# Attention with two copies of every query part: selection rows issued ahead of the moves, and all second score products over 68 rows

## The reference, cut to what matters

```
qe = einsum('hbtd,hde->hbte', q, Wq_exp) * mask      # 6 experts
ke = einsum('hbtd,hde->hbte', k, Wk_exp) * mask
attn = softmax(einsum('rbqhd,rbkhd->rbhqk', qe, ke) / D**0.5)
o = einsum('rbhqk,rbkhd->rbqhd', attn, v * mask)
o = einsum('rbthd,rbth->bthd', o, rw)                # weighted over the experts
o = (o * silu(g)) @ Wo
```

## Time and profile before

| what | us |
|---|---|
| median of 3 runs (lowest, highest) | 2963.82 (2961.93, 2968.57) |
| the profiled execution | 2963.52 |
| its span | 2961.8 |
| TensorE busy | 2509.6 (85%) |
| VectorE busy | 1791.9 (60%) |
| ScalarE busy | 1235.1 (42%) |
| GpSimd busy | 965.2 (33%) |
| DMA bytes | 441.60 MB |
| mean granted clock of TensorE | 0.914 |

### The profile page before, as it was taken

The page is one execution under the profiler, slowest core; times in us unless marked ns, Lnnn a source line. Parts: engine busy times, 40 slices in busy tenths (PEclk is TensorE's granted clock), DMA queues, the critical chain, the costliest instruction groups (busy, mean ns, idle before and its releaser), DMA issues. The chain is left out here.

```text
span 2961.8 us, 32540 instructions
## 1 busy us (share of the span) xinstructions
PE 2509.6 (85%) x9340; PEld 1655.3 (56%) x9340; DVE 1791.9 (60%) x2651; ACT 1235.1 (42%) x2450; POOL 965.2 (33%) x1004
## 2 busy tenths in 40 slices
PE   7999859999999998793799999267998865699989
PEld 5778724444444444570688888143454424588867
DVE  4310228989989998553455554448999996411143
ACT  3222027777777776231455554362233213311121
POOL 0102023333333331546100000317999994101010
PEclk9999969999999997886899999578999998899979
DMA  5253356565665661855677663634444445200031
GB/s 178 81 179 113 99 123 155 156 158 152 154 155 156 160 157 58 254 212 208 242 230 230 229 229 132 193 114 163 158 171 168 172 164 164 78 29 21 0 107 64
DMA packets 298210, 441.60 MB, mean 149 GB/s; under 512 B 41592, under 2 KB 124552, under 8 KB 298096
## 3 DMA queue, kind: packets, MB, share of 16 engines
q1 hardware_dynamic: 263392, 389.36, 43.3%
q10 hardware_dynamic: 28720, 33.10, 3.2%
q0 software_dynamic: 5984, 17.73, 1.8%
HBM read 303.85 MB, written 94.32 MB: 134 GB/s over the span
## 5 line engine op out<-in xcount | busy, mean ns | idle before, releaser
L1000 ACT ACTIVATE attn_probs<-attn_ps_score,attn_nmax 128x512 f32<-128x512 f32 x512 | 343.0, 673 | 5.6 <-DVE attn_nmax L1076 4.5
L2463 PE MATMUL scan_ps_o<-scan_qs,scan_sel 128*128 128x512 f32 x512 | 263.6, 631 | 80.5 <-DVE scan_qs L2407 53.4
L913 PE MATMUL attn_ps_score<-attn_KK,attn_S 128*128 128x512 f32 x512 | 278.8, 545 | 51.9 <-ACT attn_probs L1000 48.9
L2425 DVE TENSOR_TENSOR_SCAN scan_st<-scan_ps_dec,scan_kv 128x512 f32<-128x512 f32 x256 | 306.2, 1211 | 18.0 <-POOL scan_kv L2377 17.6
L913 PEld LDWEIGHTS attn_ps_score<-attn_KK,attn_S 128*128 128x128 f32 x512 | 101.2, 198 | 225.1 <-ACT attn_probs L1000 195.1
L841 POOL TENSOR_TENSOR attn_masked<-attn_spread,attn_q 128x512 f32<-128x512 f32 x96 | 122.7, 1281 | 294.9 <-DMA attn_spread<-rows 189.3
L2463 PEld LDWEIGHTS scan_ps_o<-scan_qs,scan_sel 128*128 128x128 f32 x512 | 88.7, 193 | 231.2 <-DVE scan_qs L2407 144.8
L1090 DVE SCALAR_TENSOR_TENSOR attn_mixed<-attn_probs,attn_cf,attn_mixed 128x512 f32<-128x512 f32 x256 | 197.2, 770 | 9.0
L1065 DVE TENSOR_REDUCE attn_raw<-attn_ps_score 128x2 f32<-128x1024 f32 x128 | 155.9, 1218 | 32.2 <-PE attn_ps_score L915 31.7
L1010 ACT ACTIVATE attn_probs<-attn_probs,attn_cf 128x512 f32<-128x512 f32 x128 | 92.4, 722 | 194.1 <-DVE attn_cf L1081 194.1
L2377 POOL TENSOR_TENSOR scan_kv<-scan_vb,gla_gk 128x512 f32<-128x512 f32 x128 | 161.2, 1277 | 19.6 <-DMA scan_vb<-gv 9.4
(11 more groups left out here) (434 smaller groups left out, 6391.3 us busy)
## 6 DMA issues: line engine op xcount, KB each, us to landing
scan_vb<-gv SPq DMA_DIRECT2D x256, 256.0 KB
moe_raw<-in_L_ffn_gating SPq DMA_DIRECT2D x92, 512.0 KB, 4.6
attn_spread<-rows SPq DMA_DIRECT2D x64, 384.0 KB, 8.8
moe_raw<-in_L_ffn_linear SPq DMA_DIRECT2D x46, 512.0 KB, 4.4
attn_S<-attn_X SPq DMA_DIRECT2D x64, 256.0 KB, 4.3
attn_S<-attn_Y SPq DMA_DIRECT2D x128, 128.0 KB, 4.3
rows_x<-out_zeros SPq DMA_DIRECT2D x23, 512.0 KB, 9.1
moe_xb<-rows_x SPq DMA_DIRECT2D x23, 512.0 KB, 5.9
```

The source lines that it names most:

```text
L913: nc.tensor.matmul(ps_score[n][:, j, :], S[p][:, 2 * n + j, cols], KK[p][:, :], start=True, stop=False)
L1000: nc.scalar.activation(probs[b][:, at_j, :], ps_score[n][:, j, :], ACT.Exp, bias=nmax[b][:, at_j:at_j + 1], accum_out=Z[b][:, at_j:at_j + ...
L2425: V.tensor_tensor_scan(st[r][:, :], ps_dec[n % 2][:, :], kv[r][:, :], 0.0, ALU.mult, ALU.add).then_inc(st_ready, 1)
L2463: nc.tensor.matmul(ps_o[w][:, :], sel[:, P - GPH - GPH * d:2 * P - GPH - GPH * d], qs[i % RING][:, :], start=(d == 0), stop=(d == HALF - 1 ...
```

## The change

The inputs of unit u + 3 are issued ahead of the mask rows and moves of u + 1. S gets two more slots, 6 and 7, for a second copy of the high parts of the shared experts; the transfer that moves a high part now always has two destinations. Partitions 64 to 67 of slots 6 and 7 are zeroed once and stay zero, so the 68-row product adds nothing there. All second products use 68 rows and S slots 4 to 7.

```diff
-        S = [m.sb(f"S{p}", [P, 6, T], F32R) for p in two]
+        S = [m.sb(f"S{p}", [P, 8, T], F32R) for p in two]
...
                 for j, half in enumerate((low, high)):
                     part = X[p][half, n, :].bitcast(F32)
-                    if n == AB:
-                        sp.dma_start(S[p][low, j:j + 5:4, :].bitcast(F32), part.unsqueeze(1).to_broadcast([DH, 2, T])
-                                     ).then_inc(sem, 16)
-                    else:
-                        sp.dma_start(S[p][low, 2 + j, :].bitcast(F32), part).then_inc(sem, 16)
+                    first_copy = 2 * n + j
+                    sp.dma_start(S[p][low, first_copy:first_copy + 5:4, :].bitcast(F32),
+                                 part.unsqueeze(1).to_broadcast([DH, 2, T])).then_inc(sem, 16)
...
             def step(i, p, u, first):
+                if left(u) >= 3:
+                    inputs(1 - p, u + 3, False)
                 if left(u) >= 1:
                     mask_rows(1 - p, u + 1, first and p == 0)
                     move(1 - p, u + 1, AB)
                     move(1 - p, u + 1, SHARED)
-                if left(u) >= 3:
-                    inputs(1 - p, u + 3, False)
                 if left(u) >= 2:
                     keys(p, u + 2, False)
...
-                ch.link(nc.gpsimd.memset(S[p][DH:DH + NSEL, 4:6, :].bitcast(F32), 0.0))
+                ch.link(nc.gpsimd.memset(S[p][DH:DH + NSEL, 4:8, :].bitcast(F32), 0.0))
...
                         nc.tensor.matmul(ps_score[n][:, j, :], S[p][:, 2 * n + j, cols], KK[p][:, :], start=True, stop=False)
-                        if n == AB:
-                            last = nc.tensor.matmul(ps_score[n][:, j, :], S[p][0:DH + NSEL, 4 + j, cols], KL[p][:, :],
-                                                    start=False, stop=True)
-                        else:
-                            last = nc.tensor.matmul(ps_score[n][:, j, :], S[p][low, 2 + j, cols], KL[p][low, :], start=False,
-                                                    stop=True)
+                        last = nc.tensor.matmul(ps_score[n][:, j, :], S[p][0:DH + NSEL, 4 + 2 * n + j, cols], KL[p][:, :],
+                                                start=False, stop=True)
```

## The result

The changed kernel takes 3026.22 us (median of 4 runs, 3014.03 to 3033.77) against 2964.38 for the kernel before in the same comparison: the ratio is 1.0204, 95% interval 1.0178 to 1.0231. It is 62 us slower. The prediction had +30 and a range that ended at 3004 (3010 for 8 in 10).

The account below looks back on a forecast made before the run. Two never-idle DMA engines, which alone carry q and k besides their share of all else, were taken to bound the attention stage. 2963.5 + 31.5 (copies) - 1 (TensorE) = 2994 us; range 2981 to 3004, for 8 in 10 2962 to 3010.

Parts of the forecast that it names:

- What bounds the kernel: Attention stage: two never-idle DMA engines, carrying q and k plus their sixteenth of all else, set 23.5 us per head.
- Part 1: Second copies of the shared experts' high parts, 2 x 128 KB more per head: 1.05 us in 30 heads, +31.5 us.
- Part 2: Inputs of head u+3 issued ahead of mask rows and moves: no byte of the two busy engines' work changes, 0 us.
- What would be late next: Moves into S would land late, so TensorE waits for S and VectorE for scores, 60 us or more; spread rows earlier.
- Part 3: TensorE's shared second products on 68 rows, 399 against 500 ns: 0 in the steady stretch, gain 0 to 2.5, taken 1 us.
- Part 4: Zeroing twice as many values of S at the start, some 1.9 us for 0.94, twice: cost 0 to 2, taken 0.
- Rival C: Attention stage: moves behind inputs leave TensorE idle at head starts, scores late by 1.45 us per head: +42, 3036; chance 0.07.
- Rival A: Attention stage: queue order is the mechanism; early spread rows end VectorE's stalls for Z: faster, 2921 to 2932 us; chance 0.13.
- the floor: One-microsecond windows of the attention stage: DMA share never under 0.12, read as two of 16 engines never idle.

Follow-up runs that it names:

- the groups: Kernel before plus 256 KB transfers by themselves, in seven groups ahead of the attention stage: 321 GB/s into 128 partitions, 205 to 208 into one half; 3043.1 us, not compared.

## Why the prediction was wrong, point by point

- What bounds the kernel: right. Two engines are never idle and a head takes their work. Splitting q and k took 2.6% off and brought heads to VectorE's 21.8 us.
- Part 1, the copies: right in mechanism and near in size. 31.5 us were predicted, 1.05 per head; the copies alone cost a ratio of 1.0103, 31 us (16 to 45), and 1.27 us per head. The profiled executions differ by 37.7 us, so that the total comes out within 1 us is in part luck: the price per head was a fifth too low. The value that I took lay just under the prices at 242 GB/s (1.08) and at the stage's average (1.07). By the slow rate that I had as the upper end, 199 GB/s, it is 1.32. The copies write one half, which in the groups was slow, and that would fit; no run shows it for the copies.
- Part 2, the order: this is the step that failed. "But the order changes no byte of the pair's work ... I take 0" is true of the bytes and false of the time. The order alone costs 0.9% and 1.44 us per head. My sum took one rate for the common work, from a trace in which it was 15.3 GB/s per engine, and carried it to another order, in which it is 13.8. That term of 0 measured 27 us by itself (18 to 35), and some 43 on top of the copies. The rows already spread from 199 to 280 GB/s at the same full share, and I used that spread only as bounds of the copies' price.
- What would be late next: wrong. I had the moves, with TensorE waiting for S. GpSimd's wait for spread rows is still the one that counts: 260.0 us, not under 50, and no wait of TensorE for S stands among its waits after 450 us. Only SyncE's wait at the mask rows is gone, as forecast. The new place gained nothing. With the order alone, where no byte is added, GpSimd's wait is 194.0 us, already more than the 164.5 of before. The estimate that the rows would land by the moves' own 6.5 us earlier took for granted that moves land just when TensorE wants them, which no row showed.
- Part 3: right for the steady stretch, mis-sized at the end. I took a gain of 1 us and at most 2.5. The end of the stage is 5.8 us shorter (62.8 to 57.0). I had counted the 2.5 us of VectorE's waits for the chosen slots' scores there; the shared slots' had another 2.6. It offset a part of the miss.
- Part 4: zeroing takes 1.8 us in place of 0.94, as predicted, and no run separates what it costs.
- Rival C had the right sign and a price near the truth (3036) with the wrong mechanism, so its price is luck: VectorE's waits for scores fell from 11.2 to 2.7 us in the changed kernel. With the order alone they rose, but only from 13.8 to 17.4 us (450 to 1180 us), and that kernel is 27 us slower by its ratio. Rival A needed the pair not to be the bound.
- The range: it took in the bounds of the copies and none for the order. With the order between 0 and the slow rate for all of the moves and spread rows (2.1 MB at 199 in place of 242 GB/s, 1.9 us per head, 57 in 30 heads) it would have reached past 3050.
- A slip without weight: between 500 and 1098 there are 598 windows, not 594. All have the floor: 95 show 0.12 or 0.13, none less.

## What to carry to other kernels

A mean DMA share of 0.60 can be a full queue: look for a floor in short windows, and for transfers like q and k here, which read rows twice by a leading dimension of 2. Here two transfers in place of each took 2.6% off the kernel. Where DMA sets the pace, the order of the transfers is not free even at equal bytes: a price per byte taken from one order holds for that order, and its spread at full share is a first estimate of the range for any move in the queue. Where one stage has a steady part and an end, price a change in both: the shorter products gave nothing in the steady part and some 6 us at the end.

## What the runs showed of the hardware that was not expected

Transfers of 256 KB, 4 or 8 in a row, that write only partitions 0 to 63, or only 64 to 127, run at 204 to 208 GB/s with all 16 engines busy, those over 128 partitions at 321. A busy share of 1.0 therefore doesn't give the rate: 199 to 321 GB/s were seen at it. The store of o, 256 KB, took SyncE 6.2 us to issue while q and k ran on two engines, and 0.40 when they were split.
